# Embedding gathers that skip repeated rows, a mask on the adds, one total and a reordered VectorE program in a retrieval-and-projection kernel

## What is computed

```python
retrieved   = jnp.mean(item_embeddings[indices], axis=1)         # [512, 512]
fused_input = jnp.concatenate([user_rep, retrieved], axis=1)     # [512, 1024]
fused_rep   = fused_input @ W_fuse + b_fuse                      # [512, 512]
logits      = fused_rep @ W_proj + b_proj                        # [512, 12500]
```

## Time and profile before

| | us |
|---|---|
| median of 3 runs | 380.3 (379.3 to 381.33) |
| the profiled execution | 380.12 |
| its span, first to last instruction | 378.3 |
| PE busy | 337.6 (89%) |
| DVE busy | 177.1 (47%) |
| POOL busy | 98.4 (26%) |
| ACT busy | 65.0 (17%) |
| mean granted TensorE clock | 0.941 of full speed |

### The profile page before, as it was taken

The page is one execution under the profiler, slowest core; times in us unless marked ns, Lnnn a source line. Parts: engine busy times, 40 slices in busy tenths (PEclk is TensorE's granted clock), DMA queues, the critical chain, the costliest instruction groups (busy, mean ns, idle before and its releaser), DMA issues.

```text
span 378.3 us, 4024 instructions
## 1 busy us (share of the span) xinstructions
PE 337.6 (89%) x1446; PEld 267.8 (71%) x1446; DVE 177.1 (47%) x268; ACT 65.0 (17%) x91; POOL 98.4 (26%) x91
## 2 busy tenths in 40 slices
PE   4997879758935995699999999999999999999996
PEld 2431878647824884488888888888888888888885
DVE  5453829872335353723635443544454445444322
ACT  1326034202000200024120222221122222220000
POOL 4778737873776157000000000000000000000000
PEclk9985689986996899899999999999999999999999
DMA  7998987895688648525784666687765755652222
GB/s 293 396 310 248 243 312 256 273 292 169 233 265 252 214 115 192 137 78 172 254 307 142 192 228 227 213 243 209 201 186 195 246 183 191 210 196 100 89 96 93
DMA packets 39388, 79.96 MB, mean 211 GB/s; under 512 B 4552, under 2 KB 32464, under 8 KB 39376
## 3 DMA queue, kind: packets, MB, share of 16 engines
q1 hardware_dynamic: 32144, 57.78, 45.8%
q0 software_dynamic: 6656, 20.98, 19.3%
q10 hardware_dynamic: 576, 1.05, 0.7%
HBM read 54.19 MB, written 25.60 MB: 211 GB/s over the span
## 4 chain that ended last, share of the span: by engine, by line
PE 60%; POOL 17%; issue 11%; DMA 6%; DVE 3%; another core or an unknown queue 1%; POOLq 1%; DVEq 0%
PE bank L557 57%; POOL ring L225 14%; DMA ring<-item_embeddings,rows 6%; PE bank L544 2%; POOL home L225 2%; DVE total L406 2%; DMA out_sb<-indices 1%; DVE out_sb L447 0%; POOL lap_row L252 0%; PE bank L535 0%; POOLq L46 0%; DVE w_lo L423 0%; DVEq L411 0%; POOLq L248 0%
## 5 line engine op out<-in xcount | busy, mean ns | idle before, releaser
L557 PE MATMUL bank<-w_hi,f_hi 128*128 (+1 forms) x400 | 159.3, 398 | 20.0 <-DVE out_sb L447 19.4
L557 PE MATMUL bank<-w_lo,f_hi 128*128 (+1 forms) x400 | 157.5, 394 | 0.0
L557 PE MATMUL bank<-w_hi,f_lo 128*128 (+1 forms) x400 | 157.1, 393 | 0.0
L447 DVE TENSOR_TENSOR out_sb<-bank,early 128x500 f32<-128x500 f32 x100 | 67.7, 677 | 124.9 <-PE bank L557 124.9
L557 PEld LDWEIGHTS bank<-w_hi,f_hi 128*128 128x128 f32 x400 | 76.6, 192 | 38.4 <-DVE out_sb L447 19.8
L225 POOL DMA_INDIRECT ring<-item_embeddings,rows x72 | 85.8, 1191 | 47.9 <-DVE total L406 23.3
L557 PEld LDWEIGHTS bank<-w_hi,f_lo 128*128 128x128 f32 x400 | 76.5, 191 | 16.0
L557 PEld LDWEIGHTS bank<-w_lo,f_hi 128*128 128x128 f32 x400 | 76.8, 192 | 15.1
L283 ACT CAST w_hi<-w_raw 128x1000 fp32r<-128x1000 f32 x50 | 51.0, 1031 | 163.9 <-DMA w_raw<-w_proj 146.2
L423 DVE TENSOR_TENSOR w_lo<-w_raw,w_hi 128x1000 fp32r<-128x1000 f32 x50 | 59.4, 1193 | 1.9 <-ACT w_hi L283 1.7
L406 DVE TENSOR_TENSOR total<-total,ring 128x1024 f32<-128x1024 f32 x26 | 31.8, 1224 | 37.1 <-DMA ring<-item_embeddings,rows 36.8
(11 more groups left out here) (45 smaller groups left out, 51.5 us busy)
## 6 DMA issues: line engine op xcount, KB each, us to landing
w_raw<-w_proj SPq DMA_DIRECT2D x50, 500.0 KB
logits<-out_sb SPq DMA_DIRECT2D x100, 250.0 KB
early<-b_proj SPq DMA_DIRECT2D x17, 250.0 KB, 5.0
ring<-item_embeddings,rows POOLq DMA_INDIRECT x72
early<-user_t ACTq DMA_DIRECT2D x4, 256.0 KB, 2.9
early<-w_fuse SPq DMA_DIRECT2D x4, 256.0 KB, 3.6
wf_ret<-w_fuse SPq DMA_DIRECT2D x1, 1024.0 KB
out_sb<-indices SPq DMA_DIRECT2D x1, 75.0 KB
```

Of the source, the lines that this page charges most:

```text
L447: nc.vector.tensor_tensor(out_sb[:, g % OUT_SLOTS, :], ps[:, 0:CHUNK], bias[:, c % BIAS_SLOTS, 0:CHUNK], ALU.add).then_inc(evacuated, 1)
L557: m = nc.tensor.matmul(ps[:, 0:CHUNK].unsqueeze(1), f[:, t, k, :], w, start=begin, stop=(f is f_lo and k == HK - 1))
```

## The change

It does five things.

1. Gathers into the ring, all but the first eight, get a bound: a row whose index is 12499 is skipped (`bounds_check`, `oob_is_err=False`), and its partition of the slot keeps its old contents. The first eight ring gathers of tile 0 are not bounded, so that a slot never holds bytes that were not written.
2. `sort` also writes a mask (1 where the index is below 12499), and every add multiplies by it: `total = ring * mask + total` (a SCALAR_TENSOR_TENSOR of 128x512). On PE, tile 0's slots are multiplied by `kept`, an identity scaled by the mask, which ACT writes at the start (`keep`, eight times 128x128).
3. One total (128x512) takes the place of two halves, and one add takes one slot. `home` takes column 0, the ring columns 1 to 17, the loop the last one: `PASSING` is 17 and `BASE` 19. The last row now comes as 128 copies (`last_rows`, 256 KB in place of 2 KB) and is multiplied by its share and put into the total by DVE (`add_last`), which for tiles 1 to 3 starts the sum and so waits until PE has turned the sum before (`ret_turned`). `count_left` takes the place of `last_means`.
4. For tile 0 DVE adds nine slots and PE eight (`DVE_FIRST`), before 14 and 4.
5. DVE's order: the first five adds of tile t + 1 (`AHEAD`) stand ahead of `fused_lo(t)`, the other twelve, two at a time, ahead of the evacuations of groups 0 to 5 of tile t, and `add_home` behind add 14. `sort(3)` moves ahead of tile 0's projections.

```diff
-PASSING = 18
+PASSING = 17
-PE_SLOTS = 4
+DVE_FIRST = 9
+PE_FIRST = PASSING - DVE_FIRST
+AHEAD = 5
+HOME_AFTER = 14
...
-            sp.dma_start(last_col[:], last_item).then_inc(last_landed, 16)
+            sp.dma_start(last_rows[:], last_item.to_broadcast([P, H])).then_inc(last_landed, 16)
...
                 u, j = q // PASSING, q % PASSING
-                if j >= 2 * pairs(u):
-                    pool.wait_ge(slot_summed, j - 2 * pairs(u) + 1)
+                if u == 0 and j == PASSING - 1:
+                    pool.wait_ge(ret_turned, 1)
+                elif u == 0 and j >= DVE_FIRST:
+                    pool.wait_ge(slot_summed, j - DVE_FIRST + 1)
                 else:
-                    pool.wait_ge(added, adds_done(u, max(1, j // 2)))
+                    pool.wait_ge(added, adds_done(u, j))
...
-                gather(home[:], rows[:, t, PASSING:STATIC]).then_inc(home_landed[t], 16)
+                gather(home[:], rows[:, t, 0:1]).then_inc(home_landed[t], 16)
...
+                    skip = {} if t == 0 and i < RING else {"bounds_check": LAST - 1, "oob_is_err": False}
+                    gather(ring[:, place(t, i), :], rows[:, t, i + 1:i + 2], **skip)\
+                        .then_inc(slot_landed[place(t, i)], 16)
...
+            def add(t, i):
+                here = ring[:, place(t, i), :]
+                dve.wait_ge(slot_landed[place(t, i)], 16 * slot_uses(t, i))
+                if t == 0 and i == 0:
+                    nc.vector.tensor_scalar(total[:], here, mask[:, 0, 1:2], None, ALU.mult).then_inc(added, 1)
+                    return
+                if i == 0:
+                    dve.wait_ge(last_added, t + 1)
+                elif t and i == HOME_AFTER + 1:
+                    dve.wait_ge(home_added, t + 1)
                 else:
+                    dve.wait_ge(added, adds_done(t, i - 1))
+                nc.vector.scalar_tensor_tensor(total[:], here, mask[:, t, i + 1:i + 2], total[:],
+                                               ALU.mult, ALU.add).then_inc(added, 1)
...
+            for t in range(TILES):
+                fused_lo(t)
                 for c in range(RESIDENT):
+                    if t + 1 < TILES and c < RESIDENT - 2:
+                        add_pair(t + 1, AHEAD + 2 * c)
+                        if AHEAD + 2 * c + 1 == HOME_AFTER:
+                            add_home(t + 1)
+                    if t == 0 and c < 4:
+                        split_lo(c + 4)
+                    if t + 2 < TILES and c >= RESIDENT - 2:
+                        if c == RESIDENT - 2:
+                            add_last(t + 2)
+                        add_pair(t + 2, 2 * (c - RESIDENT + 2))
...
                     evacuate(t, c)
+                if t + 2 < TILES:
+                    add(t + 2, 4)
```

More of the change, by code:

```diff
@@ L59, in retrieval_scores @@
         home = sb("home", [P, H])
-        total = sb("total", [P, 2, H])
+        total = sb("total", [P, H])
         early = sb("early", [P, 2, HK, 512])
@@ L143, in slot_uses, with adds_done @@
             return (PASSING * t + i) // RING + 1
-        def pairs(t):
-            return (PASSING - (PE_SLOTS if t == 0 else 0)) // 2
-        def adds_done(t, j):
-            return sum(pairs(u) for u in range(t)) + j
+        def adds_done(t, i):
+            return (DVE_FIRST + PASSING * (t - 1) if t else 0) + i + 1
         def group_of(t, c):
@@ L269, in _ @@
                     place_free(t, i)
-                    gather(ring[:, place(t, i), :], rows[:, t, i:i + 1]).then_inc(slot_landed[place(t, i)], 16)
+                    skip = {} if t == 0 and i < RING else {"bounds_check": LAST - 1, "oob_is_err": False}
+                    gather(ring[:, place(t, i), :], rows[:, t, i + 1:i + 2], **skip)\
+                        .then_inc(slot_landed[place(t, i)], 16)
         @block.scalar
@@ L304, in fused_hi @@
                                          bias=bf_col[:, n:n + 1]).then_inc(f_hi_ready, 1)
+            act.wait_ge(ident_ready, 1)
+            act.wait_ge(mask_ready, 1)
+            for i in range(PE_FIRST):
+                keep(i)
             split_hi(0)
@@ L380, in last_means @@
                 dve.wait_ge(n_left_ready, 1)
                 dve.wait_ge(last_landed, 16)
-                for t in range(TILES):
-                    nc.vector.tensor_scalar(last_mean[:, t, :], last_col[:], n_left[:, t:t + 1], None, ALU.mult)\
-                      .then_inc(last_mean_ready, 1)
-            def wait_pair(t, j):
-                for i in (2 * j, 2 * j + 1):
-                    dve.wait_ge(slot_landed[place(t, i)], 16 * slot_uses(t, i))
-            def pair(t, j):
-                p = place(t, 2 * j)
-                return ring[:, p:p + 2, :]
@@ new lines, in add_last @@
+            def add_last(t):
+                share = n_left[:, t:t + 1]
+                if t == 0:
+                    dve.wait_ge(added, adds_done(0, DVE_FIRST - 1))
+                    nc.vector.scalar_tensor_tensor(total[:], last_rows[:], share, total[:], ALU.mult, ALU.add)\
+                      .then_inc(last_added, 1)
+                    return
+                dve.wait_ge(ret_turned, t)
+                nc.vector.tensor_scalar(total[:], last_rows[:], share, None, ALU.mult).then_inc(last_added, 1)
@@ L413, in add_home @@
                 dve.wait_ge(home_landed[t], laps * 16)
[L414 to L418 removed]
+                nc.vector.tensor_tensor(total[:], total[:], home[:], ALU.add).then_inc(home_added, 1)
             def split_lo(c, halves=(0, 1)):
@@ L456, in _ @@
             sort(1)
-            add_pair(0, 1)
+            for i in range(5):
+                add(0, i)
             count_columns()
-            add_pair(0, 2)
-            last_means()
+            add(0, 5)
+            add(0, 6)
             split_lo(0, (0,))
-            add_pair(0, 3)
+            add(0, 7)
+            count_left()
+            add(0, 8)
+            add_last(0)
+            dve.wait_ge(laps_ready, 1)
             split_lo(0, (1,))
-            add_pair(0, 4)
             split_lo(1, (0,))
-            add_pair(0, 5)
+            add_home(0)
@@ L587, in _ @@
             pe.wait_ge(n_left_ready, 1)
-            for i in range(2 * pairs(0), PASSING):
-                if i == PASSING - 2:
-                    pe.wait_ge(added, adds_done(0, pairs(0)))
-                    sum_in(total[:, 0, :])
-                    sum_in(total[:, 1, :])
+            for i in range(DVE_FIRST, PASSING):
+                if i == PASSING - 1:
+                    pe.wait_ge(home_added, 1)
+                    sum_in(total[:], ident[:])
+                pe.wait_ge(kept_ready, i - DVE_FIRST + 1)
                 pe.wait_ge(slot_landed[place(0, i)], 16 * slot_uses(0, i))
-                m = sum_in(ring[:, place(0, i), :], first=(i == 2 * pairs(0)), last=(i == PASSING - 1))
-                m.then_inc(slot_summed, 1)
+                m = sum_in(ring[:, place(0, i), :], kept[i - DVE_FIRST], first=(i == DVE_FIRST), last=(i == PASSING - 1))
+                m.then_inc(slot_summed if i < PASSING - 1 else ret_turned, 1)
             fuse(0)
```

124 lines of the change are left out of this document (50 added, 74 removed).

## The result

The changed kernel took 364.58 us (364.07 to 364.79, 4 runs) beside 380.39 of the kernel before: ratio 0.960, 95% interval 0.955 to 0.965. Times are medians of all executions, and ratios are estimated without the slow ones, so that a ratio can differ from the quotient of two medians. I had forecast 350.0, in a range of 342 to 366. The direction was right. About half of the forecast gain, 14.6 us of 30, was missing. Its profiled execution took 364.79 us with a span of 363.0.

What follows compares the result with a forecast made beforehand. PE bounds the last 77 groups; before them POOL's late gathers make PE wait. `turn_sum(3)` at 129 + 217.8 + 1.4 = 348.2 of span, +1.8 gives 350 us, range 342 to 366 (8 in 10).

Steps and rivals of the forecast that it cites:

- 129 with 1.4 added: Start of `turn_sum(3)`: PE ready at 129 us, POOL's last landing at 130.8, so 1.4 us added to PE's time.
- The waits of POOL ahead of gather 8: POOL's standstill once per tile, 4.79, 5.84 and 10.43 us before, forecast to fall under 2 us.
- 217.8: Microseconds behind the last transposition that stay: transposition, half a group, fuse, 77 groups, evacuation and store.
- tile 0's sum: Nine slot sums on PE from 34.3 to 44.2 us; fuse(0) then starts at 46.7 instead of 49.41, -2.7 us.
- the 2.1 us: Idle time between PE's end at 46.84 and ACT's start at 48.90 in the kernel before, kept unexplained.
- a gap of 2.02 us: PE's gap before tile 0's seventh group, forecast to stay, from splits, loads and casts of chunks 6 and 7.
- adds in front: Rival: adds ahead of f_lo wait for landings and DVE may keep POOL out; 361 us together, chance 0.25.
- 79 + 1.1 + 0.45 + 4.2 for the fuse + 0.7 = 85.5: PE's step from `turn_sum(1)` at 79 us through the fuse to tile 1's first group at 85.5 us.
- The skipping: nothing: Skipping 34% of 21 MB of gathered rows gains nothing in the sum, since POOL's 1.25 us ignores bytes.
- Bounded gather 1.59 or 1.89: Rivals: POOL needs 1.59 us per bounded gather, 377 us, chance 0.05; or 1.89 us, 390 us, chance 0.04.
- skips nothing: Rival: bounded gathers fetch all rows anyway, so only landings behind a busy DMA suffer; 353 us.
- The odd row: The 8.29 us gather at 24.55, read as DVE keeping POOL out of SBUF; 5 us taken back.

Runs made afterwards that it cites:

- after_third: The changed kernel itself, run again unedited on chip 0 as the control of its batch: 351.33 us, ratio 0.939 to the kernel before.
- before_again: The kernel before, unedited, run again and profiled on chip 15: 379.90 us, ratio 0.991 to itself.
- no_skip: The changed kernel without bounds on its gathers, so every row is moved, masks kept, on chip 10: 367.41 us, ratio 0.966 to the kernel before.

## Why the prediction was right and wrong

On a chip that posts on time, every step stands within 1.4 us of where I put it (forecast, after_third): fuse(0) 46.7, 47.14; first group 52.8, 53.83; `turn_sum(1)` 79, 77.94; first group of tile 1 85.5, 84.53; `turn_sum(2)` 103, 102.28; `turn_sum(3)` 129 with 1.4 added, 130.07; time 350, 351.33. The waits of POOL ahead of gather 8 went; the 77 groups and what lies around them took 219.1 us from `turn_sum(3)` on in either state (363.0 - 143.86; 349.2 - 130.07), where I had 217.8.

Part of this is luck. Two errors cancel in tile 0's sum. I let it start 2.1 us after the last two spreadings of the biases, though the row has 3.69 us for them; they began at 32.18, as forecast, and the sum at 35.81, not 34.3. And I took 1.1 of the nine sums at the lower clock, but the granted clock was 0.51 from 35.8 to 41.3, with PE busy since 32.18, and 1.00 from there to the sum's end. So the sum ended at 46.68, 2.5 us behind my 44.2, and the 2.1 us between it and ACT that I kept were not there. Then the first group came 1.0 us later than in my sum, and tile 0's groups, in which I kept a gap of 2.02 us that was 0.20 here, took 2.1 us less. That the first measurement, 364.58 us, lies in the range of 342 to 366 is luck too: it is in there for a rival, adds in front, that did not come about.

**The step that failed** is the one from the fuse to the first group of the next tile: "79 + 1.1 + 0.45 + 4.2 for the fuse + 0.7 = 85.5". It took increments to be there when the matmul is over. Set beside after_third, the profiled execution lost 1.7 us up to `turn_sum(1)` (79.60 for 77.94; the late posting of tile 0's sum), 6.8 from there to the first group of tile 1 (13.35 for 6.59), 2.3 in that tile's groups (20.08 for 17.75; the granted clock was 0.50 for the first 4.05 us and 1.00 throughout in after_third), and 1.5 twice more up to `turn_sum(3)`: 13.8 in all, which is the difference of the spans. That late posting costs this is read from the steps at which two chips differ with one kernel; no run took it away on a late chip at no other cost.

**What I should have read.** The sign was in my own rows: the 2.1 us between PE's end at 46.84 and ACT's start at 48.90, which says "remote". I kept it as a constant, "unexplained". On chip 0 it is gone (ACT starts at 46.72, released by PE), and it is one case of late posting. The change keeps POOL issuing through the fuses, which in the kernel before fell in its long waits. My rivals asked only what POOL's gathers do to POOL and DVE, not to PE's announcements.

**The gain.** Even on chip 0 it is 23.7 us, not 30: the kernel before is 5 us faster there (375.04 for 380.39). Late posting is not shown to be the cause of these 5 us: the kernel before has no trace on chip 0, its late traces show only some 2 us of it at tile 0's sum, and its fastest executions on chips 14 and 15 (373.4 and 371.5 us) are near those of chip 0 (371.9). My sum started from 380 of a late execution, rebuilt the time ahead of `turn_sum(3)` from steps that hold no late posting but the 2.1 us, and so ended at the time of an on-time one.

**Smaller terms.** A gather with a bound costs 1.00 us, not 0.95. The masked add costs 0.75, not 0.70. Both were hidden. "The skipping: nothing" was wrong by 3 to 4 us on late chips; what it saves is not POOL's time but the landing of weights in tile 0. It was not measured on chip 0. A gather's own landing got no shorter with fewer rows: 4.9 us from issue in the middle case there, 2.3 to 7.2 at the ends, for 4.8. Adds in front of `f_lo` held it up by what the sum had for them and no more. On chip 0 the last row, five adds and two splits run from 46.82 to 53.34, 6.5 us for my 6.4, and `f_lo(0)` stands right behind them, 2.96 us after `f_hi` began at 50.38; DVE in after_third:

```profile
46.82 0.49 DVE L423 TENSOR_SCALAR total<-last_rows,n_left 128x512 f32<-128x512 f32 x1 [9.90 <-PE bank L543]
...
52.68 0.74 DVE L412 SCALAR_TENSOR_TENSOR total<-ring,mask,total 128x512 f32<-128x512 f32 x1
53.34 1.12 DVE L444 SCALAR_TENSOR_TENSOR f_lo<-bank,bf_col,f_hi 128x128 fp32r<-128x128 f32 x4
```

DVE stood at none of these adds for a landing, so the rival at 361 did not come about, though its number did. "Bounded gather 1.59 or 1.89" and "skips nothing" fall with the rows.

**The odd row.** The 8.29 us gather came back as 7.97 us at 25.45 in before_again; in the changed kernel the longest gather into the ring took 1.96 us, and beside DVE's dense run from 46.82 to 53.34 on chip 0 the longest took 1.70. So the dense adds did not keep POOL out for long: those gathers took up to 0.7 us over their 1.00. The exception in the Trainium skill (SBUF — State Buffer, Who interferes with whom) is stated for a tensor_tensor and called inferred there; the new adds fit it, while the row of the kernel before stays against it. What caused that row wasn't tried.

**Left open.** How posting can be late at all, and why on three chips or more and not on the fourth. POOL's gathers go with it: no fuse whose first increment came over 1.4 us behind the last gather was late, and nothing was late behind the kernel's last gather. But they alone don't suffice: with as dense gathers chip 0 has none late, and on chip 14 tile 1's fuse passed with 0.7 us. Nor does a release need a pause: of 94 releases of increments over 0.5 us late, 58 fell while a gather was still running. Traffic of stores and the number of increments were tried and are not it.

A second difference goes with the first. In each of the 13 late traces, 53 to 109 of the 509 to 554 increments of all engines have no record; in the seven of chip 0 none is missing. So the recording of increments may itself have a part in their lateness. That rival is not tested: no run without the recording is on hand. Nor is it shown that the chip decides, and not the way in which the program was loaded: chip 0 was used in two batches, the others in one each.

No version beats the changed kernel on a chip that posts on time. On a late one none that computes the whole result does by more than can be measured.

## What to carry to other kernels

An idle stretch whose releaser the profile doesn't know is a cost with a cause of its own: before it is kept as a constant, ask what else ran then, and whether the change brings the same company to places that had none. A change that keeps a queue busy all the time takes away the pauses in which others got through. And before an edit gets the credit, run the unchanged kernel in the same batch: here the chip was worth 10 to 13 us, about as much as the best single part of the change, and one early increment (`left_spread`) told which kind of chip it was.

## What the runs showed of the hardware

- TensorE's semaphore increments can come up to 8 us after the matmul that carries them, several in one burst 42 ns apart, while those of other engines are on time (4329 recorded in the 13 late traces, none over 0.02 us late). They were seen on chips 10, 14 and 15 in every trace, in the kernel before too (4.2 us at `left_spread`), and on chip 0 in none of seven. None was seen behind the last gather of GpSimd (1114 recorded).
- An indirect gather of 128 rows with a bound occupies POOL for 1.00 us, without one for 0.95; skipping the rows out of bounds cut the gather queue's bytes from 19.9 (no_skip) to 13.9 MB; the kernel before, with one column more, moved 21.0.
- Two rows say how much the lower clock costs: the same first matmul of a group took 0.76 us after 8.28 idle us (92.95 in the changed kernel's first profile, granted clock 0.50), 0.46 after 1.79 (84.53 in after_third, granted clock 1.00).
